# A graph layer on one core: two small products cut into parts, the first chunk prepared alone, transfers and layer norm steps re-timed

## The reference, cut to what matters

```python
# x (10000, 128), adj (10000, 10000), item_feat (10000, 128), all float32
h = jnp.maximum(_layernorm(x, axis=-1), 0.0)
def _L0_gnn_ref(user_feat, item_feat, adj, W_item, b_item, W_user, b_user):
    h = item_feat @ W_item.T + b_item
    b = user_feat @ W_user.T + b_user
    return jax.nn.relu(adj @ h + b)
x = x + _L0_gnn_ref(h, item_feat, adj, W_item, b_item, W_user, b_user)
```

## Time and profile before

| | us |
|---|---|
| median of 3 runs | 1099.3 (1099.22 to 1101.26) |
| the profiled execution | 1099.5 |
| its span, first to last instruction | 1097.7 |

### The profile page before, as it was taken

One profiled execution on the slowest core, in us unless ns is written; L12 is line 12 of the kernel. 1 busy time (PEld: TensorE's weight loads), 2 busy tenths in 40 slices (PEclk: granted clock), 3 DMA queues, 4 the chain that ended last, 5 costly groups with the idle time before them and its releaser, 6 DMA issues.

```text
span 1097.7 us, 12056 instructions
## 1 busy us (share of the span) xinstructions
PE 1090.9 (99%) x4964; PEld 898.1 (82%) x4964; DVE 969.6 (88%) x620; ACT 758.9 (69%) x474; POOL 30.8 (3%) x61
## 2 busy tenths in 40 slices
PE   9999999999999999999999999999999999999998
PEld 7788788888888888888878888888788888888887
DVE  7899989999989898889898988898989888998986
ACT  6677777667777676666776666777676667677763
POOL 0000000000000000000000000000000000000000
PEclk9999999999999999999999999999999999999999
DMA  9999999999999999999999999999999999999993
GB/s 371 416 426 426 421 353 392 365 369 402 425 384 402 361 396 370 386 391 422 415 393 365 403 370 370 414 425 396 392 366 390 376 366 395 403 399 384 372 365 129
DMA packets 64599, 421.56 MB, mean 384 GB/s; under 512 B 7960, under 2 KB 8876, under 8 KB 24608
## 3 DMA queue, kind: packets, MB, share of 16 engines
q1 hardware_dynamic: 59840, 406.21, 92.7%
q0 software_dynamic: 4416, 14.45, 4.8%
q10 hardware_dynamic: 288, 0.13, 0.0%
HBM read 415.64 MB, written 5.12 MB: 383 GB/s over the span
## 4 chain that ended last, share of the span: by engine, by line
PE 97%; DMA 1%; SPq 1%; DVE 0%; issue 0%; DVEq 0%
PE acc L608 31%; PE acc L615 31%; PE acc L609 31%; PE acc L580 2%; PE acc L549 1%; DMA items<-in_item_t 1%; PE acc L590 0%; SPq L231 0%; SPq L259 0%; SPq L258 0%; SPq L255 0%; DVE y L481 0%; PE acc L572 0%; PE acc L566 0%; DVEq L124 0%
## 5 line engine op out<-in xcount | busy, mean ns | idle before, releaser
L391 DVE TENSOR_TENSOR lo_ring<-a_ring,hi_ring 128x2048 fp32r<-128x2048 f32 (+1 forms) x381 | 849.2, 2236 | 99.5 <-ACT hi_ring L325 98.1
L325 ACT CAST hi_ring<-a_ring 128x2048 fp32r<-128x2048 f32 (+1 forms) x381 | 713.9, 1874 | 314.5 <-PE acc L615 292.0
L608 PE MATMUL acc<-hi_ring,h_lo 128*128 128x512 f32 (+1 forms) x1560 | 611.4, 392 | 0.5 <-DVE h_lo L413 0.5
L615 PE MATMUL acc<-lo_ring,h_hi 128*128 128x512 f32 (+1 forms) x1560 | 600.5, 385 | 0.0
L609 PE MATMUL acc<-hi_ring,h_hi 128*128 128x512 f32 (+1 forms) x1560 | 599.7, 384 | 0.0
L608 PEld LDWEIGHTS acc<-hi_ring,h_lo 128*128 128x128 f32 x1560 | 293.0, 188 | 65.1 <-issue 8.6
L609 PEld LDWEIGHTS acc<-hi_ring,h_hi 128*128 128x128 f32 x1560 | 293.1, 188 | 61.6 <-issue 4.6
L615 PEld LDWEIGHTS acc<-lo_ring,h_hi 128*128 128x128 f32 x1560 | 292.8, 188 | 60.4 <-DVE lo_ring L391 1.1
L406 DVE TENSOR_TENSOR h_full<-acc,bi 128x384 f32<-128x384 f32 x26 | 14.4, 554 | 17.6 <-PE acc L549 11.0
L281 POOL DMA_DIRECT2D y<-in_x_t x20 | 10.8, 540 | 563.8 <-ACT hi_ring L325 563.8
L549 PEld LDWEIGHTS acc<-wi,items 128*128 128x128 f32 x156 | 21.8, 196 | 4.2 <-DMA items<-in_item_t 1.9
(11 more groups left out here) (31 smaller groups left out, 95.6 us busy)
## 6 DMA issues: line engine op xcount, KB each, us to landing
a_ring<-in_adj_tiles SPq DMA_DIRECT2D x312, 1024.0 KB, 7.8
a_ring<-in_adj_tiles SPq DMA_DIRECT2D x78, 904.0 KB, 6.5
rows<-in_x_slices POOLq DMA_DIRECT2D x19, 256.0 KB, 7.2
y<-in_x_t POOLq DMA_DIRECT2D x19, 256.0 KB, 6.6
items<-in_item_t SPq DMA_DIRECT2D x12, 384.0 KB, 10.8
out_t<-y POOLq DMA_DIRECT2D x16, 256.0 KB, 7.3
out_t<-y SPq DMA_DIRECT2D x3, 256.0 KB, 2.4
a_rem<-in_adj_rem SPq DMA_DIRECT2D x19, 32.0 KB, 8.0
```

The costliest lines, as they stand in the source:

```text
L325: nc.scalar.copy(hi_ring[:, n % S_SLOTS, cols], a_ring[:, n % A_SLOTS, cols]).then_inc(hi_written, 1)
L391: nc.vector.tensor_tensor(lo_ring[:, s, cols], a_ring[:, s, cols], hi_ring[:, r, cols], ALU.subtract).then_inc(lo_written, 1)
L608: nc.tensor.matmul(acc[k][:, 0:bank_w(g, k)], h_lo[:, c, :], hi, start=(c == 0), stop=False, skip_group_check=True)
L615: last = nc.tensor.matmul(acc[k][:, 0:bank_w(g, k)], h_hi[:, c, :], lo, start=False, stop=(c == CHUNKS - 1), skip_group_check=True)
```

## The change

It has these parts.

1. **User product in parts.** From group 1 on the normalised and transposed x is split like a tile: ScalarE rounds it into `turned_hi`, VectorE subtracts into `turned_lo`, and TensorE does three fp32r products with `wu_lo` and `wu_hi`. In group 0 it stays as it is.
2. **Left-over product in parts.** The 16 left-over rows are loaded three times, with two rows of ones, as 50 rows per bank; ScalarE rounds them, VectorE subtracts in the last 16; the weights hold h_hi, h_lo, h_hi and the bias as hi and lo. One fp32r matmul per bank gives all three products. Banks lie in pairs at rows 0 and 64.
3. **First chunk of h ahead.** Chunk 0 goes to a bank of its own and is summed, rounded and subtracted alone; chunks 1 and 2 follow inside tile 0. `wi` and `bi` come in one transfer. The warm-up behind the first trio has 4 products instead of 8.
4. **Transfers.** The small ones go ahead of tile 18 instead of behind tile 7, items piece 2 ahead of tile 6, the left-over rows ahead of tile 30 instead of 12, the rows of x in group 0 at tiles 14, 16, 18, 20 instead of 5, 10, 15, 20.
5. **Parts of tiles.** Tiles 0 and 1 in quarters, tiles 2 to 11 in halves, instead of tiles 0 to 8 in quarters.
6. **Layer norm re-timed**, with one table for group 0 and one for the later groups.

The core of the diff:

```diff
-SUM_AT = 14
 SUM_EVERY = 2
-MEAN_AT = 23
-NORM_AT = 57
-USER_AT = 59
...
+FIRST = {"sum": 22, "mean": 30, "centre": 32, "square": 35, "sum_squares": 36, "wide_every": 4, "var": 51, "eps": 54, "sqrt": 57,
+         "root": 58, "norm": 59, "user": 61, "rem_round": 50, "rem_subtract": 52, "rem": 66}
+LATER = {"sum": 6, "mean": 15, "centre": 18, "square": 21, "sum_squares": 22, "wide_every": 5, "var": 40, "eps": 43, "sqrt": 46,
+         "root": 47, "norm": 50, "turned": 53, "turned_lo": 54, "user": 57, "rem_round": 38, "rem_subtract": 40, "rem": 66}
...
+            def turned_round(g, k):
+                u, v, n = g * UNITS + k, (g - 1) * UNITS + k, bank_w(g, k)
+                act.wait_ge(normed_t_ready, u + 1)
+                if v >= 2:
+                    act.wait_ge(user_done, u - 1)
+                nc.scalar.copy(turned_hi[:, v % 2, 0:n], columns_of(normed_t)[:, 0:n]).then_inc(turned_hi_set, 1)
...
+            def turned_subtract(g, k):
+                u, v, n = g * UNITS + k, (g - 1) * UNITS + k, bank_w(g, k)
+                dve.wait_ge(turned_hi_set, v + 1)
+                if v > 0:
+                    dve.wait_ge(user_done, u)
+                nc.vector.tensor_tensor(turned_lo[:, 0:n], columns_of(normed_t)[:, 0:n], turned_hi[:, v % 2, 0:n],
+                                        ALU.subtract).then_inc(turned_lo_set, 1)
...
+            def user_parts(g, k):
+                u, v, n, out = g * UNITS + k, (g - 1) * UNITS + k, bank_w(g, k), acc_of(g)[k]
+                pe.wait_ge(turned_hi_set, v + 1)
+                nc.tensor.matmul(out[:, 0:n], wu_lo[:, :], turned_hi[:, v % 2, 0:n], start=False, stop=False, skip_group_check=True)
+                nc.tensor.matmul(out[:, 0:n], wu_hi[:, :], turned_hi[:, v % 2, 0:n], start=False, stop=False, skip_group_check=True)
+                pe.wait_ge(turned_lo_set, v + 1)
+                nc.tensor.matmul(out[:, 0:n], wu_hi[:, :], turned_lo[:, 0:n], start=False, stop=False,
+                                 skip_group_check=True).then_inc(user_done, 1)
...
                 for k in range(ACC_BANKS):
-                    rows_k = slice(k * ROWS_BLOCK, k * ROWS_BLOCK + REM + 1)
-                    last = nc.tensor.matmul(acc_of(g)[k][:, 0:bank_w(g, k)], h_rem[rows_k, :], a_rem[rows_k, 0:bank_w(g, k)],
+                    row, n = k % PAIR * ROWS_BLOCK, bank_w(g, k)
+                    rows_k = slice(row, row + REM_ROWS)
+                    last = nc.tensor.matmul(acc_of(g)[k][:, 0:n], h_rem[rows_k, :], rem_parts[rows_k, k // PAIR, 0:n],
```

More of the change, by code:

```diff
@@ L53 @@
 S_SLOTS = 4
-ROWS_BLOCK = 32
-REM_AFTER = 12
+PAIR = 2
+ROWS_BLOCK = 64
+REM_ROWS = 3 * REM + 2
+REM_HI = 2 * REM
+DMA_SCRATCH = 8192
+REM_AFTER = 30
 TRIO = 3
@@ L363, in _ @@
                 for c in range(CHUNKS):
-                    if g == 0 and c < SPLIT_TILES:
-                        for part in range(ACC_BANKS):
+                    parts = parts_of(g, c)
+                    if parts > 1:
+                        for part in range(parts):
                             if c == 0 and part == 0:
+                                h_first_round_hi()
+                            if c == 0 and part == 2:
                                 h_round_hi(0)
-                            round_part(c, part)
+                            round_part(c, part, parts)
                     else:
@@ L487, in _ @@
                 for c in range(CHUNKS):
-                    if g == 0 and c < SPLIT_TILES:
-                        for part in range(ACC_BANKS):
+                    parts = parts_of(g, c)
+                    if parts > 1:
+                        for part in range(parts):
                             if c == 0 and part == 0:
+                                h_first_subtract_lo()
+                            if c == 0 and part == 3:
                                 h_subtract_lo(0)
-                            subtract_part(c, part)
-                            if c == 1 and part == 1:
+                            subtract_part(c, part, parts)
+                            if c == 1 and part == parts // 2 - 1:
                                 h_add_bias(1)
@@ L548, in h_trio @@
                     at = part * TRIO_W + m * P
-                    last = nc.tensor.matmul(bank[:, m * HID:(m + 1) * HID], items[:, slot, at:at + P], wi[:, :],
-                                            start=(m == 0), stop=True, skip_group_check=True)
+                    out = h_rem_bank[:, 0:HID] if trio == 0 and m == 0 else bank[:, m * HID:(m + 1) * HID]
+                    last = nc.tensor.matmul(out, items[:, slot, at:at + P], wi,
+                                            start=(m == 0 or (trio, m) == (0, 1)), stop=True, skip_group_check=True)
+                    if trio == 0 and m == 0:
+                        last.then_inc(h_first_done, 1)
                 last.then_inc(h_done, 1)
@@ L671 @@
     left[:N_USER] = adj[:, full:]
+    left_rows = np.ones((GROUPS * ACC_BANKS, REM_ROWS, BANK_W), np.float32)
+    for part in range(3):
+        left_rows[:, part * REM:(part + 1) * REM] = left.reshape(GROUPS * ACC_BANKS, BANK_W, REM).transpose(0, 2, 1)
     x_padded = np.zeros((GROUPS * GROUP_W, HID), np.float32)
@@ L675 @@
         "adj_tiles": tiles.reshape(GROUPS, GROUP_W, CHUNKS, P).transpose(0, 2, 3, 1).reshape(GROUPS * CHUNKS, P, GROUP_W),
-        "adj_rem": left.reshape(GROUPS * ACC_BANKS, BANK_W, REM).transpose(0, 2, 1),
-        "ones_row": np.ones((1, BANK_W), np.float32),
+        "adj_rem": left_rows,
         "item_t": np.asarray(L0_gnn_item_feat).T,
```

300 lines of the change are left out of this document (213 added, 87 removed).

## The result

The changed kernel takes 1091.6 us (median of 4 runs, 1091.45 to 1091.86) where the kernel before, on the same chip, takes 1099.3 (1099.1 to 1101.26): a ratio of 0.993, interval 0.9917 to 0.9942. The profiled execution took 1091.6, with a span of 1089.8. The forecast was 1091.1.

A forecast was written before the change was run, and what follows sets the result against it. TensorE, busy 1090.9 of 1097.7 us, was taken as the bound, with arrivals deciding early on. Gains of 3.3 + 2.1 + 2.8 = 8.2 us took 1099.3 to 1091.1; range 1088.0 to 1095.8.

The forecast's parts named there:

- User product, 3.3: Groups 1 to 4: three fp32r products replace one f32 product, gaining 0.20 us for each of 16 units, 3.3 in all.
- Left-over product, 2.1: Each of five groups: four fp32r matmuls in pairs on two strips take 0.86 us instead of 1.28, gain 2.1.
- not together, in the plain stream: Left-over product: case where the four fp32r matmuls do not overlap and follow at the plain step, 0.91 us.
- Start, 1.3: First product of tile 0: earlier bias and chunk 0 prepared alone let it start at 7.1 instead of 8.36, gain 1.3 us.
- cover, not path: Start: four warm-up products fewer end at about 6.8 instead of 7.8 us, which was to give slack but no time.
- Items piece, waits, transfers: First 40 us: items wait of 1.5 us and 1.0 of other waits go; with the start 2.8, from 1.3 to 3.8.
- (a) of the prediction: Tile 2: with halves instead of quarters, the first lo half comes about 0.5 us late behind an h rounding on ScalarE.
- What costs nothing: Added VectorE and ScalarE work stays hidden: VectorE needs 13.1 of 14.3 us per five tiles, with 2.6 us of lead.
- Rival 1: Start and first 30 tiles: the start gives nothing, waits reappear at tiles 12 to 30; 1093.4 us, chance 0.14.
- Rival 2: User parts of later groups: VectorE becomes the bound and the kernel slower, 1112 us at 2.5 us of waiting; chance 0.06.
- Rival 3: Left-over product: fp32r on two strips is no faster than f32 on four, stays at 1.3 us; 1093.2 us, chance 0.15.
- Rival 4: Plain tiles: TensorE's step changes with the rings' new place in memory, 3.9 us per 0.01 us per tile; chance 0.05.

The follow-up runs named there:

- the kernel with both edits of the start: Tiles 0 to 2 in quarters and 7 warm-up products ahead of the h products instead of 5, against the changed kernel: 1091.5 us.

## Why the prediction was right, point by point

**User product, 3.3.** The sum held: undoing it costs 3.5, of which 0.3 is the earlier place, so 3.2 in the change. Its parts did not hold. Per unit 0.16, not 0.20, since the three records stand 0.23 to 0.24 apart and the first plain one behind them 0.24, the delay that I had put at the low end. That makes 2.6; about 0.7 came from the tiles of group 4, which no row I had read pointed to. Two errors of opposite sign: that the sum came out is luck.

**Left-over product, 2.1.** 1.28 to 0.87 is 0.41, times 5 is 2.0. The size held. The records do start in pairs, as forecast, but with the order of the strips changed they do so too and the time stays, so pairs on two strips are not confirmed as the reason. The inside is also different: rounds of 0.33 instead of 0.21, and 0.2 instead of 0.43 at the ends. The value 0.91 for "not together, in the plain stream" was as near, and I had no row to choose between them.

**Start, 1.3.** 1.10 at the first product. Tile 0 landed on time, and the weights' longer transfer ate into the cover as foreseen. Missed: tile 0 itself, which took 3.98 instead of 3.65. The four warm-up products fewer, put down as "cover, not path", were path: with eight the first product starts at 8.52, so at the first product this edit carries the gain of the start as much as the bias does. In the medians the two are worth 0.4 and 0.6.

**Items piece, waits, transfers; 2.8 with the start.** The first product of tile 24 came at 80.78 instead of 83.54, 2.76 earlier, which looks like a hit. But 0.26 of it is the product for the means, which now stands behind tile 24, and at tile 36 the gain is 2.48; with the 0.4 of the left-over product that makes group 0's end. The same product was counted as a wait in the forecast. Of the 1.1 us between 28.80 and 83.11 that were left to win, 0.26 was this product and 0.26 the slow h product right behind the items wait (0.69 to tile 6, 0.43 at tile 24), so the waits of tiles 6 to 24 that went were 0.5, not 1.0. Tile 5 with the items wait gave 1.7, not 1.5. The halves in tile 2 cost 3.82 - 3.31 = 0.51, as in (a) of the prediction, and three tiles in quarters gives it back (3.31). Wrong in size: the left-over rows, put at 0.7 us more for 400 instead of 128 KB. By the rates they take 2.2 instead of 0.8, 1.4 more, and by the arrival of tile 12 they take 3.1. It did no harm where the change puts them, ahead of tile 30; ahead of tile 12 they would have cost 2.4. So moving them was not one of several small gains: with their new size it was needed.

**What costs nothing.** Held: no wait for `lo_ring` in the later groups. By the estimate above there was room for about 2 us more of VectorE work per unit.

**Rivals.** Rival 1 fell with tile 24; its mechanism, that arrivals set the time, is what holds back the kernel with both edits of the start. Rival 2 came about only with four more subtractions per unit. Rival 3 fell, 0.87 against 1.28. Rival 4 fell: a plain tile of groups 1 to 3 takes 2.720 as before.

**Sum.** Forecast 3.3 + 2.1 + 2.8 = 8.2. By the traces it is 3.2 + 2.0 + 2.5 = 7.7, and the medians differ by 7.6. The group was to be 1.2 shorter and is 1.04: the user units again. Not tried: the layer norm's new places alone, and the left-over product in its old form in this kernel.

## What to carry to other kernels

When an engine is full, price a replaced operation by the distance between its neighbours' starts, ahead and behind, and look also at the plain work that follows it for the rest of the stage. Where the queues are full, bound a small transfer by the rate that the queues show while it is under way, not by its bytes alone. Early in a kernel a gain ahead of an arrival only holds until that arrival: find the last late one before counting it. When a gain is read at one tile, see that the same work stands ahead of that tile in both kernels. And when a kernel's executions scatter, compare their mean granted clock before explaining the median from one trace.
